# Expert results scattered to eight places for each token, summed in sixteen steps, and rotated banks for the shared product

## The reference, cut to what matters

```
scores = sigmoid(x @ gate_w.T)                        # 32 experts in 4 groups
topi   = the 8 best experts of the 2 best groups      # for each token
wsel   = scores[topi] / sum(scores[topi]) * 2.5
x_lat  = x @ fc1_w.T                                  # 512 -> 256
h      = relu(x_lat @ w1[e].T) ** 2 * weight of e     # 256 -> 256, for each of the 8 experts e
y_lat  = sum over the 8 experts of h @ w2[e].T        # 256 -> 256
out    = x_in + relu(x @ up.T) ** 2 @ down.T + y_lat @ fc2_w.T
```

## Time and profile before

| | us |
|---|---|
| median of 3 runs (1148.5 to 1149.4) | 1148.77 |
| the profiled execution | 1156.29 |
| its span, first to last instruction | 1154.5 |
| PE busy | 1066.4 (92%) |
| DVE busy | 689.7 (60%) |
| POOL busy | 550.3 (48%) |
| ACT busy | 511.2 (44%) |
| share of PE in the chain that ended last | 70% |
| PE waiting for a DMA of `sums` at the start of the tail | 12.4 |

### The profile page before, as it was taken

The page is one execution under the profiler, slowest core; times in us unless marked ns, Lnnn a source line. Parts: engine busy times, 40 slices in busy tenths (PEclk is TensorE's granted clock), DMA queues, the critical chain, the costliest instruction groups (busy, mean ns, idle before and its releaser), DMA issues.

```text
span 1154.5 us, 13537 instructions
## 1 busy us (share of the span) xinstructions
PE 1066.4 (92%) x4126; PEld 646.1 (56%) x4127; DVE 689.7 (60%) x1326; ACT 511.2 (44%) x770; POOL 550.3 (48%) x433
## 2 busy tenths in 40 slices
PE   0479999999999999999999999999999999999948
PEld 0334444444444444545444344448999999999934
DVE  8997549999999999823892000004444444444435
ACT  3465435666565745331211111106656656665501
POOL 3523004513451446200047666654777777777730
PEclk9989999999999999999999999999999999999979
DMA  4563024524541537303015755276887887888687
GB/s 154 161 206 98 1 37 138 161 80 124 176 152 49 166 98 223 81 9 127 19 40 205 255 180 209 100 249 140 144 139 135 143 140 136 139 143 138 97 213 258
DMA packets 126032, 157.71 MB, mean 137 GB/s; under 512 B 8992, under 2 KB 104224, under 8 KB 125984
## 3 DMA queue, kind: packets, MB, share of 16 engines
q1 hardware_dynamic: 94688, 113.63, 32.9%
q0 software_dynamic: 31296, 43.53, 19.9%
HBM read 79.67 MB, written 77.46 MB: 136 GB/s over the span
## 4 chain that ended last, share of the span: by engine, by line
PE 70%; DVE 17%; issue 9%; DMA 1%; another core or an unknown queue 1%; ACT 1%; POOL 1%; POOLq 0%; ACTq 0%; DVEq 0%; SPq 0%
PE banks L1624 23%; PE banks L616 12%; PE banks L627 12%; PE banks L547 9%; PE banks L570 7%; PE banks L603 3%; PE banks L525 2%; DVE arena L1373 2%; PE banks L1639 1%; DVE arena L1364 1%; DVE arena L1362 1%; DVE arena L1475 1%; DVE arena L1466 1%; DVE arena L1502 1%
## 5 line engine op out<-in xcount | busy, mean ns | idle before, releaser
L1624 PE MATMUL banks<-arena 128*128 128x512 f32 x896 | 390.4, 596 | 12.0 <-DVE arena L1427 5.2
L1624 PEld LDWEIGHTS banks<-arena 128*128 128x128 f32 x896 | 170.8, 191 | 228.4 <-issue 217.2
L487 POOL DMA_INDIRECT sums<-arena x160 | 249.5, 1560 | 82.1 <-DVE arena L889 54.3
L475 POOL DMA_INDIRECT slots_in<-arena x128 | 129.2, 1010 | 103.7 <-issue 84.4
L889 DVE TENSOR_TENSOR arena<-banks,arena 128x512 f32<-128x512 f32 x80 | 55.3, 691 | 172.3 <-PE banks L627 172.3
L616 PE MATMUL banks<-arena 128*128 128x128 f32 x1280 | 156.1, 275 | 0.4 <-ACT arena L728 0.3
L627 PE MATMUL banks<-arena 128*128 x640 | 151.1, 379 | 0.0
L616 PEld LDWEIGHTS banks<-arena 128*128 128x128 f32 x1280 | 149.3, 192 | 0.8 <-issue 0.8
L547 PE MATMUL banks<-arena 128*128 128x512 f32 x320 | 144.2, 598 | 0.7 <-ACT arena L755 0.7
L627 PEld LDWEIGHTS banks<-arena 128*128 128x128 f32 x640 | 115.6, 190 | 12.5
L570 PE MATMUL banks<-arena 128*128 128x512 f32 x256 | 115.4, 594 | 6.1 <-DVE arena L932 6.1
(11 more groups left out here) (181 smaller groups left out, 1205.2 us busy)
## 6 DMA issues: line engine op xcount, KB each, us to landing
slots_in<-arena SPq DMA_DIRECT2D x20, 1120.0 KB, 6.0
arena<-slots_in SPq DMA_DIRECT2D x80, 280.0 KB
arena<-fT SPq DMA_DIRECT2D x32, 256.0 KB, 3.0
arena<-w2T SPq DMA_DIRECT2D x4, 2048.0 KB
arena<-sums SPq DMA_DIRECT2D x16, 512.0 KB, 8.7
sums<-arena SPq DMA_DIRECT2D x4, 1152.0 KB, 5.8
arena<-xT SPq DMA_DIRECT2D x4, 1024.0 KB, 8.6
arena<-xT POOLq DMA_DIRECT2D x4, 1024.0 KB, 9.7
```

What stands on the lines that cost most here:

```text
L475: pool.indirect_dma_start(rows_in, bass.IndirectOffsetOnAxis(ap=POSU[:, n, j:j + 1], axis=0), XLR[:, n], None).then_inc(S['scattered'], 16)
L487: pool.indirect_dma_start(sums[g % RING], bass.IndirectOffsetOnAxis(ap=DESTU[:, g:g + 1], axis=0), YO[:, i % 4, c], None, compute_op=ALU.add)\
L1624: ins = pe.matmul(out, w[:, k, m * P:(m + 1) * P], x[:, k], start=(k == 0), stop=(k == kt - 1))
```

## The change

In the shared stage, `DOWN_BANK` becomes a table with four other banks for each token block, and the first `down` matmul into a bank waits for the evacuation that last used it, one or two blocks back. One more wait (`routed`) keeps banks 5 and 6 free for the routing.

The results of the experts are no longer added in DRAM. A token's row now carries, instead of its number, eight destinations (`TO`), one for each of its experts. `meta` picks weight and destination with one mask, and POOL writes the 128 rows of a block to 128 different rows of a tensor `parts` (plain indirect DMA, no ring, no wait but the copy's). Rows that belong to no token are written where nothing reads them. The tensors `sums` and their zeroing are gone.

The tail goes in 16 steps of 128 tokens. `parts` holds a token's eight results one after the other, so a load brings 8 KB to each partition. DVE adds eight to four and four to two; PE adds the last two while it turns them, as two products with the identity into one bank; ACT copies, PE multiplies by `fc2` into one bank for all four tiles, DVE adds to `XN`, and SP stores 128 tokens of all 512 channels. Loads are issued six steps ahead of the stores.

The diff, cut to its core:

```diff
-    sums = [nc.dram_tensor(f"sums{r}", [B * T + P, LAT], F32).ap() for r in range(RING)]
+    parts = nc.dram_tensor("parts", [(SLOT_BLOCKS + B * T * TOPK // P) * P, LAT], F32).ap()
...
-            for r in range(RING):
-                sp.wait_ge(y_added[r], 16 * (NB // RING))
-                if r == 0:
-                    sp.wait_ge(S['m1_mm'], NP)
-                load_sums(0, r)
-            for b in range(1, B):
-                for r in range(RING):
-                    load_sums(b, r)
...
+            def load_parts(g):
+                at = (SLOT_BLOCKS + g * TOPK) * P
+                of = slice(at, at + TOPK * P)
+                sp.dma_start(YB[:, g], parts[of].rearrange("(p j) d -> p j d", j=TOPK)).then_inc(parts_loaded[g], 16)
+
+            sp.wait_ge(S['m2_mm'], NP)
+            for q in range(4):
+                sp.wait_ge(y_sent[q], 32 * (NP // 4))
+            AWAY = 6
+            for g in range(AWAY):
+                load_parts(g)
+            for g in range(NT):
+                if g + AWAY < NT:
+                    load_parts(g + AWAY)
+                b, tt = divmod(g, TT)
+                of = slice(tt * P, (tt + 1) * P)
+                sp.wait_ge(S['out_ready'], g + 1)
+                sp.dma_start(view(A['out'], b)[:, :, of], XN[:, b, :, of]).then_inc(S['out_stored0'], 16)
...
-                    if g >= RING:
-                        pool.wait_ge(y_added[g % RING], 16 * (g // RING))
-                    pool.indirect_dma_start(sums[g % RING], bass.IndirectOffsetOnAxis(ap=DESTU[:, g:g + 1], axis=0),
-                                            YO[:, i % 4, c], None, compute_op=ALU.add)\
-                        .then_inc(y_added[g % RING], 16)
-        DOWN_BANK = (2, 3, 4, 7)
+                    pool.indirect_dma_start(parts, bass.IndirectOffsetOnAxis(ap=DESTU[:, g:g + 1], axis=0),
+                                            YO[:, i % 4, c], None).then_inc(y_sent[i % 4], 16)
+        DOWN_BANK = ((2, 3, 4, 7), (5, 6, 2, 3), (4, 7, 5, 6), (2, 3, 4, 7))
...
-                    if k == 0 and b:
-                        pe.wait_ge(S['down_evac'], K * (b - 1) + m + 1)
+                    if k == 0 and b == 1 and m == 0:
+                        pe.wait_ge(S['routed'], 1)
+                    if k == 0 and b and DOWN_BANK[b][m] in DOWN_BANK[b - 1]:
+                        pe.wait_ge(S['down_evac'], K * (b - 1) + DOWN_BANK[b - 1].index(DOWN_BANK[b][m]) + 1)
+                    elif k == 0 and b >= 2:
+                        pe.wait_ge(S['down_evac'], K * (b - 2) + DOWN_BANK[b - 2].index(DOWN_BANK[b][m]) + 1)
...
-            pe.wait_ge(sums_loaded[0][1], 16)
+            pe.wait_ge(S['fc2_loaded'], 16)
+            pe.wait_ge(y_sent[(NP - 1) % 4], 32 * (NP // 4))
...
+            def latent(g):
+                pe.wait_ge(S['combined'], g + 1)
+                if g >= 2:
+                    pe.wait_ge(S['yT_ready'], g - 1)
                 for k in range(KL):
+                    for r in range(2):
+                        ins = pe.matmul(bank(3 + g % 2)[:, k * P:(k + 1) * P], YB[:, g, r, k * P:(k + 1) * P], IDENT,
+                                        start=(r == 0), stop=(r == 1))
...
+            for g in range(NT):
+                if g + 1 < NT:
+                    latent(g + 1)
+                fc2(g)
...
+                mask = EQP[:, q % 2].rearrange("p c (o j) -> p c o j", o=1).to_broadcast([P, 2, 2, TOPK])
+                step.did(dve.tensor_tensor(EQW[:, q % 2], both, mask, ALU.mult))
                 step.wait()
+                step.did(dve.tensor_reduce(WTO[:, mine], EQW[:, q % 2], AX.X, ALU.add))
+                step.wait()
+                dve.scalar_tensor_tensor(DESTU[:, mine], SLOT[:, mine], -1.0, WTO[:, mine, 1], ALU.add, ALU.max)\
+                   .then_inc(S['meta_ready'], 1)
...
-                        sp.wait_ge(S['zero_ready'], 2)
+                        sp.wait_ge(S['zero_ready'], 1)
                     if nxt:
                         zero_slots(8 * b + n - 4 if prev else n)
-                    else:
-                        zero_sums(n // 2, n % 2)
```

More of the change, by code:

```diff
@@ L293, in build @@
         JCOL = place(NT)
+        TO = place(NT, TOPK)
         ICOL = place(NB)
@@ L297, in build @@
         top[0] = kept
[L298 to L302, removed]
+        YB = place(NT, TOPK, LAT)
         assert top[0] <= end2
@@ L324, in build @@
         after = top[0]
+        top[0] = end2
+        YL = place(4, KL, P)
         top[0] = end2
@@ L694, in part2_pe, with fc2 @@
-            pe.wait_ge(S['y_copied'], NP)
-            pe.wait_ge(S['fc2_loaded'], 16)
+                    for r in range(2):
+                        ins = pe.matmul(bank(3 + g % 2)[:, k * P:(k + 1) * P], YB[:, g, r, k * P:(k + 1) * P], IDENT,
+                                        start=(r == 0), stop=(r == 1))
+                ins.then_inc(S['yT_mm'], 1)
+            def fc2(g):
+                pe.wait_ge(S['yT_ready'], g + 1)
+                if g >= 2:
+                    pe.wait_ge(S['out_ready'], g - 1)
+                for m in range(K):
+                    for k in range(KL):
+                        ins = pe.matmul(bank(1 + g % 2)[:, m * P:(m + 1) * P], FC2[:, k, m * P:(m + 1) * P], YL[:, g % 4, k],
+                                        start=(k == 0), stop=(k == KL - 1))
+                ins.then_inc(S['fc2_mm'], 1)
@@ L749, in part2_act @@
                     own_w1(i + 2)
-            for b in range(B):
-                for k in range(KL):
-                    act.wait_ge(S['yT_mm'], KL * b + k + 1)
-                    if k == 0 and b >= 2:
-                        act.wait_ge(S['fc2_mm'], 4 * (b - 1))
-                    act.activation(YL[:, b % 2, k], bank(3 + 2 * (b % 2) + k), ACT.Copy).then_inc(S['yT_ready'], 1)
+            for g in range(NT):
+                act.wait_ge(S['yT_mm'], g + 1)
+                if g >= 4:
+                    act.wait_ge(S['fc2_mm'], g - 3)
+                act.activation(YL[:, g % 4].rearrange("p k t -> p (k t)"), bank(3 + g % 2)[:, 0:KL * P], ACT.Copy)\
+                   .then_inc(S['yT_ready'], 1)
         def part2_dve(dve, step):
@@ L901, in part2_dve, with combine, out @@
             result(NP - 1)
[L903 to L927 removed]
+            def combine(g):
+                dve.wait_ge(parts_loaded[g], 16)
+                dve.tensor_tensor(YB[:, g, 0:4], YB[:, g, 0:4], YB[:, g, 4:8], ALU.add).then_inc(S['halved'], 1)
+                dve.wait_ge(S['halved'], g + 1)
+                dve.tensor_tensor(YB[:, g, 0:2], YB[:, g, 0:2], YB[:, g, 2:4], ALU.add).then_inc(S['combined'], 1)
+            def out(g):
+                b, tt = divmod(g, TT)
+                of = XN[:, b, :, tt * P:(tt + 1) * P]
+                dve.wait_ge(S['fc2_mm'], g + 1)
+                dve.tensor_tensor(of, of, bank(1 + g % 2).rearrange("p (m t) -> p m t", m=K), ALU.add).then_inc(S['out_ready'], 1)
+            for g in range(NT):
+                combine(g)
+                if g >= 2:
+                    out(g - 2)
+            out(NT - 2)
+            out(NT - 1)
         def down_tile(dve, b, m):
```

100 lines of the change are left out of this document (19 added, 81 removed).

## The result

| | us |
|---|---|
| before, in the same runs | 1148.78 (1148.5 to 1149.4) |
| changed kernel, median of 4 runs | 1157.41 (1156.96 to 1159.34) |
| ratio, 95% interval | 1.0078 [1.006, 1.0095] |
| its profiled execution, and its span | 1156.96, 1155.4 |
| PE, DVE, ACT, POOL busy in it | 1082.2, 717.8, 512.8, 455.2 |

The kernel is 8.6 us slower; I had forecast 3.2 us slower. Direction and range held, the size did not. Busy time says little of it: PE rose by 16 us, but POOL fell by 95.

The account below looks back on a forecast made before the run. PE was taken to bound the shared and expert stages, DMA the new tail. From 1148.77 us, -9.1 (banks) and +11.9 (tail) gave +2.8, rounded up to +3.2: 1152.0 us, range 1146 to 1162.

Parts of the forecast that it names:

- Banks rotated: Shared stage: PE no longer stalls at first down products of token blocks 1 to 3; -9.1 us, lower bound 0.2.
- B: End of shared stage: POOL's scatters end at 777 whatever PE does, so rotated banks give nothing; 1160.9 us, chance 0.13.
- The tail: End of kernel: last scatters, 16 larger loads of parts with stores among them, last sums and product; +11.9 us.
- The sum: Whole kernel: -9.1 us from the banks and +11.9 in the tail give +2.8, rounded up to +3.2: 1152.0 us.
- DMA bounds a step: Tail: a step takes 3.34 us of DMA against 2.8 on DVE and 2.7 on PE, bound by half a microsecond.
- A: Tail: loads of parts stay at 348 GB/s, the rate of sums; +8.3 us, 1160.3 us, chance 0.15.
- C: Tail: PE's clock stays at half in every step, 16 steps take 86 us; 1187.9 us, chance 0.04.
- D: Tail: stores beside loads cost the queue nothing, steps go at DVE's pace; 4.0 us less, 1144.8 us, chance 0.16.
- Scatter without an add: Expert stage, POOL: 0.97 us for a plain scatter against 1.56 for a scatter-add, hidden under PE's 3.95 a pair.
- Zeroing gone: Between 390 and 452 us: 8.9 MB of stores dropped, beside PE work that waits for no DMA; worth nothing.

## Why the prediction was right in direction and wrong in size

*Banks rotated, -9.1 us:* this step failed. It took three stalls of one execution, and a product at half clock behind the first, for the kernel's. The text itself had the warning, 7.5 us between the profiled execution and the median, and set it aside as an offset. Where the evacuations are on time there is no stall to save (ratio 1.0 with the rotation alone, 48 timed executions of before at 1151.9 us or less); where they are late, POOL's scatters end late as well and take the gain back (0.9991). The argument against B, that POOL stops at the same moments as ACT and so would move with PE, was wrong: both wait for the same signal, but the signal is late by itself, not because PE is. B had a chance of 0.13; its mechanism was right where signals are late. Its 0.2 us for the term agrees with both runs, whose intervals reach 2.1 us and 4.4 us of gain.

*The tail, +11.9 us:* measured 65.0 - 54.1 = +10.9 in the pair compared. The forecast for the new tail alone was 65.7, and its terms held but for the first: from the last copy to the first load 4.9 us (6.2 forecast: the issue came 1.5 us after the last scatter's end, not 2.5, and the last two copies lay 1.7 us apart, not 1.4); issue to last landing 49.8 (49.8: the seven loads ahead of the first store landed 2.5 us apart and the nine behind it mostly 3.1 to 3.2, against the 2.49 and 0.85 a store that I had; with all loads first it was 43.3, so the stores are 6.5 of it, where I had 7.7); behind it 10.3 (9.7). That the median moved by 8.6 and not 10.9 lies in the kernel before, whose tail is 54.1 in one profile and 57.1 in another of the same instructions on the same chip: 65.0 - 57.1 = 7.9. The 2 us by which the last copy came earlier in the pair compared (1090.4 against 1092.4) are there before the change begins to act: 1.7 of them arise between 127 and 140 us, where the clock was at half in the one profile (0.57 over 127 to 131) and at full in the other.

*The sum:* the forecast was 5.4 us too low, and this is the difference of two errors. The banks made it 9.1 too low. The tail made it 3.7 too high: 0.7 since the new tail is 65.0 and not 65.7, the rest, as far as the profiles show, since I took the tail of before from the profile in which it is shortest. The direction was right because 11.9 is more than 9.1; that the total stayed inside the range owes something to luck.

*DMA bounds a step:* right for the end of the tail. Warm clock and half the turns gave nothing, half the bytes 4.2 us. But PE was closer than "half a microsecond", 2.79 us against the queue's 3.2, and after a slow start nine intervals between steps went at its pace before the queue caught up.

*A (348 GB/s):* wrong; 423 over 27 us in the run with all loads first. The Trainium skill (DMA: Bandwidth & Descriptors, Specifications) gives some 358 GB/s of HBM to a core and 435 to the fabric. These traces agree with the second alone.

*C (half clock throughout):* wrong as a whole, right for one piece: the clock was at 0.50 to 0.74 from 1102 to 1108, with idle times of PE of 1.87 and 1.14 us in and ahead of this stretch, and one product took 3.33 us. The run with warm PE, which ended no sooner, shows that this cost nothing at the end.

*D (stores beside loads):* wrong; the stores cost 6.5 us of the queue.

*Scatter without an add:* 0.97 us as forecast, on POOL, hidden. *Zeroing gone:* no sign of a gain; the stretch was not tested alone.

## What to carry to other kernels

Before a stall of a profile goes into a sum, hold the profiled execution against the timed ones: where it is longer by as much as the stall is worth, profile again. The same holds for the stretch that is compared: the tail of before differed by 3 us between two profiles, a third of what the change cost. A wait that one engine loses can be held by another that hears the same signal late, so follow every waiter for it to the end of the stage. Replacing an add in DRAM by eight plain places doubles the bytes behind the last write, and this is paid in the tail at the DMA rate, unless the places are half as wide.

## What the runs showed of the hardware that I had not expected

- The same kernel takes 1148.6 and 1148.9 us on two chips and 1160.0 and 1160.8 on two others. On the latter, other engines hear late of PE's progress during the shared stage: POOL went on 5.3 to 11.0 us after the product that it waited for, against 0.8 to 0.9 us ("remote" in the rows, where the profile knows no event that released them). The first profile of before has the same late rows, at 1156.29 us. Whether it comes from the chip, and what carries the delay, stays open; nothing that I ran tells it.
- On one chip the same instructions differ by 2.6 us up to the first scatter of rows and by 3.0 us in the tail, and the granted clock (0.57 against 1.00 from 127 to 131 us; in the tails 0.50 from 1110 to 1115 us against 1.00 from 1112 to 1118) differs with them.
- Loads of 8 KB rows ran at 423 GB/s for 27 us, those of 1 KB rows at 348.
- A plain scatter of 128 rows landed 2.4 us after its start, and the chain's last scatter-add, with the first loads of `sums` already under way, 6.0 us (the scatter-adds of that profile landed in 3.6 to 6.0 us, 4.0 in the median):

```profile
1092.79 2.41 DMA parts<-arena
```

```profile
1098.77 5.99 DMA sums<-arena
```
